# The moments of a residual one slot later, and the row scale behind the first four maxima of the next graph

## The reference

```
q, k, v = x @ Wq.T, x @ Wk.T, x @ Wv.T + bv            # split into 12 heads
scores  = q k^T * 384**-0.5 + (adj + adj)
scores  = where(any(scores != 0, over keys), scores, -inf)
p       = nan_to_num(softmax(scores))
out     = (p @ v) @ Wo.T + bo
result  = layernorm(x + out)                           # no gain, no shift
```

## Time and profile before

| | us |
|---|---|
| median of 3 runs (lowest, highest) | 638.47 (637.63, 639.18) |
| the profiled execution | 637.14 |
| its span, first to last instruction | 635.4 |
| PE, DVE, ACT, POOL busy | 593.0, 482.7, 497.6, 452.6 |
| mean granted TensorE clock | 0.993 |

### The profile page before, as it was taken

How to read it: one execution, slowest core, us unless ns; L and a number is a source line. 1 busy time by engine, 2 the same in 40 slices (tenths; PEclk the granted TensorE clock), 3 DMA queues, 4 the chain that set the end, 5 groups by cost and what they waited for, 6 DMA issues and landing times.

```text
span 635.4 us, 23731 instructions
## 1 busy us (share of the span) xinstructions
PE 593.0 (93%) x8448; PEld 518.5 (82%) x8448; DVE 482.7 (76%) x2380; ACT 497.6 (78%) x1975; POOL 452.6 (71%) x691
## 2 busy tenths in 40 slices
PE   8899999999999999999999999999999999999773
PEld 5788888888888888888888888888878888888663
DVE  4778877877877877877877877777887787787884
ACT  5688778778788778778878877877878878877882
POOL 1577777777687687778768678777768768667773
PEclk9999999999999999999999999999999999999998
DMA  8311324232142422224242132423214222112221
GB/s 305 134 37 46 109 85 137 75 110 84 47 134 87 125 84 64 95 82 135 84 126 81 39 121 86 132 80 91 91 58 135 86 75 86 52 52 86 87 79 50
DMA packets 34749, 59.63 MB, mean 94 GB/s; under 512 B 10568, under 2 KB 24008, under 8 KB 34632
## 3 DMA queue, kind: packets, MB, share of 16 engines
q1 hardware_dynamic: 34200, 57.53, 28.1%
q10 hardware_dynamic: 432, 0.59, 0.3%
HBM read 44.50 MB, written 13.62 MB: 91 GB/s over the span
## 4 chain that ended last, share of the span: by engine, by line
PE 74%; DVE 19%; issue 3%; DMA 3%; ACT 0%; POOLq 0%; POOL 0%; DVEq 0%
PE qk_ps L339 32%; PE scores_ps L430 16%; PE v_ps L373 15%; PE scores_ps L360 9%; DVE y L639 6%; DVE stats L642 5%; DVE att_n L626 5%; DMA scale_t<-scale_mem 2%; PE scores_ps L442 1%; DMA scale_mem<-scale_rows 1%; DMA x_raw<-xt 1%; DVE nscores L558 1%; DVE mean_var L644 0%; PE v_ps L442 0%; PE qk_ps L442 0%
## 5 line engine op out<-in xcount | busy, mean ns | idle before, releaser
L473 ACT ACTIVATE probs<-nscores,neg_max 128x128 f32<-128x128 f32 x768 | 297.5, 389 | 34.7 <-DVE neg_max L558 34.7
L287 POOL TENSOR_TENSOR tree<-nscores 128x512 f32<-128x512 f32 (+1 forms) x128 | 143.1, 1118 | 115.1 <-DVE neg_max L558 115.1
L558 DVE CUSTOM_DVE_ANT_0 nscores<-scores_ps,adj_n 128x128 f32<-128x128 f32 x768 | 171.9, 286 | 4.0 <-PE scores_ps L360 1.7
L473 ACT ACTIVATION_READ_ACCUMULATOR probs<-nscores,neg_max 128x1 f32 x768 | 144.0, 187 | 0.0
L287 POOL TENSOR_TENSOR tree<-tree 128x128 f32<-128x128 f32 (+2 forms) x256 | 127.8, 499 | 20.1
L639 DVE TENSOR_TENSOR y<-scores_ps,x_n 128x384 f32<-128x384 f32 x64 | 35.7, 558 | 110.2 <-PE scores_ps L430 110.2
L430 PE MATMUL scores_ps<-w_o,att_t 128*128 128x384 f32 x576 | 112.8, 341 | 7.1 <-DVE att_t L630 4.6
L373 PE MATMUL v_ps<-w_v,x_t 128*128 128x384 f32 x576 | 111.7, 338 | 1.1 <-ACT probs_t L498 1.1
L339 PE MATMUL qk_ps<-x_t,w_k 128*128 128x512 f32 (+1 forms) x540 | 108.9, 346 | 0.0
L373 PEld LDWEIGHTS v_ps<-w_v,x_t 128*128 128x128 f32 x576 | 102.2, 188 | 7.4 <-ACT probs_t L498 1.9
L339 PE MATMUL qk_ps<-x_t,w_q 128*128 128x512 f32 (+1 forms) x540 | 107.5, 343 | 0.0
(11 more groups left out here) (71 smaller groups left out, 928.0 us busy)
## 6 DMA issues: line engine op xcount, KB each, us to landing
x_n<-xn SPq DMA_DIRECT2D x32, 384.0 KB, 4.8
scale_t<-scale_mem SPq DMA_DIRECT2D x63, 192.0 KB
out<-out_n SPq DMA_DIRECT2D x31, 384.0 KB, 2.6
x_raw<-xt SPq DMA_DIRECT2D x15, 768.0 KB, 5.4
adj_n<-adj SPq DMA_DIRECT2D x32, 128.0 KB, 4.4
scale_mem<-scale_rows SPq DMA_DIRECT2D x63, 16.0 KB
x_raw<-xt SPq DMA_DIRECT2D x3, 256.0 KB, 4.8
nscores<-wq ACTq DMA_DIRECT2D x3, 192.0 KB, 4.2
```

What stands on the lines that cost most here:

```text
L287: nc.gpsimd.tensor_tensor(tree[:, b % 2, low:high, 0:width], src[:, :, 0:width], src[:, :, width:2 * width], ALU.add).then_inc(tree_step, 1)
L473: last = nc.scalar.activation(probs[:, b % 2, h], nscores[:, b % 2, h], ACT.Exp, bias=neg_max[:, b % 2, h:h + 1], scale=-1.0, accum_out=ro ...
L558: last = nc.vector.tensor_tensor_reduce(out=nscores[:, half, h], in0=scores_ps[j][:, m * P:(m + 1) * P], in1=adj_n[:, b // 2 % 2, half], s ...
```

## The change

Three edits, all on VectorE:

- The two instructions that find the moments of y leave `residual(b)` and become `moments(b)`, called one slot later, behind `find_scale`. The last two graphs have theirs right behind their residuals.
- `bias_and_max(b + 1, 0)`, the first four maxima of the next graph, comes ahead of `find_scale(b)`.
- `total` and `nonzero` are views with a stride of two elements of buffers twice as long.

```diff
-        total = sb("total", [P, HEADS])
-        nonzero = sb("nonzero", [P, HEADS])
+        total = sb("total", [P, HEADS, 2])[:, :, 0]
+        nonzero = sb("nonzero", [P, HEADS, 2])[:, :, 0]
...
                 nc.vector.tensor_tensor(y[:, half], out_bank(b)[:, 0:HID], x_n[:, b // 2 % 2, half],
                                         ALU.add).then_inc(y_ready, 1)
+
+            def moments(b):
+                half = b % 2
                 dve.wait_ge(y_ready, b + 1)
                 nc.vector.bn_stats(stats[:], y[:, half]).then_inc(stats_done, 1)
                 dve.wait_ge(stats_done, b + 1)
...
             for b in range(-1, NB + 1):
                 if has(b - 1):
                     normalise(b - 1)
+                if has(b + 1):
+                    bias_and_max(b + 1, 0)
                 if has(b):
                     find_scale(b)
+                if has(b - 2) and has(b):
+                    moments(b - 2)
                 if has(b + 1):
-                    bias_and_max(b + 1, 0)
                     bias_and_max(b + 1, 1)
                 if has(b - 1):
                     attention_low(b - 1)
...
                         residual(b - 1)
                 elif b == NB:
                     residual(b - 2)
+                    moments(b - 2)
                     residual(b - 1)
+                    moments(b - 1)
```

More of the change, by code:

```diff
@@ L588, in find_scale @@
                 dve.wait_ge(tree_step, STEPS * (b + 1))
-                nc.vector.reduce_sum(total[:], tree[:, half, :, 0:REST], axis=mybir.AxisListType.X).then_inc(total_done, 1)
+                nc.vector.reduce_sum(total, tree[:, half, :, 0:REST], axis=mybir.AxisListType.X).then_inc(total_done, 1)
                 dve.wait_ge(total_done, b + 1)
-                nc.vector.scalar_tensor_tensor(out=nonzero[:], in0=neg_max[:, half], scalar=0.0, in1=total[:],
+                nc.vector.scalar_tensor_tensor(out=nonzero, in0=neg_max[:, half], scalar=0.0, in1=total,
                                                op0=ALU.not_equal, op1=ALU.max).then_inc(nonzero_done, 1)
@@ L601, in find_scale @@
                         out=scale_n[:].rearrange("p (h d) -> p h d", h=HEADS),
-                        in0=nonzero[:].unsqueeze(2).to_broadcast([P, HEADS, D]), scalar=0.0,
+                        in0=nonzero.unsqueeze(2).to_broadcast([P, HEADS, D]), scalar=0.0,
                         in1=recip[:].unsqueeze(2).to_broadcast([P, HEADS, D]),
@@ L608, in find_scale @@
                 nc.vector.scalar_tensor_tensor(out=row_scale[:, 0:HEADS].rearrange("p (j m) -> p m j", m=KT),
-                                               in0=nonzero[:].rearrange("p (m j) -> p m j", m=KT), scalar=0.0,
+                                               in0=nonzero.rearrange("p (m j) -> p m j", m=KT), scalar=0.0,
                                                in1=recip[:].rearrange("p (m j) -> p m j", m=KT),
```

## The result

The changed kernel takes 718.85 us (median of 4 runs, 718.26 to 722.14) against 638.05 before: a ratio of 1.128, 95% interval 1.125 to 1.132. Two more comparisons of the same pair gave 716.42 (1.122, interval 1.120 to 1.124) and 716.19 (1.121, 1.115 to 1.127). The forecast was 700 with a range of 688 to 715, so the direction and the cause held and the size did not: 62 us were forecast and 81 (78 and 78 in the repeats) came.

What follows compares the result with a forecast made beforehand. The loop through DRAM was taken as the bound: 3.81 + 6.53 = 10.34 us a slot, +58.8 us over 62 intervals, +2.0 head, +0.7 end, giving a span of 696.9 and a time of 700 us; range 688 to 715.

Steps and rivals of the forecast that it cites:

- TensorE's slot is 9.10 us of its own work: Steady slot before the change: 9.47 us, of which 9.10 is TensorE's work and 0.37 waiting for VectorE.
- The scale behind four maxima closes a loop through DRAM that becomes the bound: att_n, scores, four maxima, scale, write, read, att_n: 10.34 us a slot, above TensorE's 9.10, also in the last slots.
- The terms outside the trip, 3.81 us: From att_n to the write's issue: 1.72 us to the maxima, 0.85 for four maxima, 1.24 for find_scale.
- The round trip, 6.53 us: From the issue of the scale's write to DRAM until att_n: 6.85 us in odd slots, 6.2 in even ones.
- the first rival: Write and read through DRAM take longer in steady slots: slot 10.86 us, 732 us; chance 0.09 together with the strides.
- Head and end: First scale later by 2.0 us at the start; moments of graph 61 uncovered in slot 63, 0.7 us.
- The moments give back at most 0.37 us a slot, seen if the loop is open: Moments leave the stretch between y and att_n: at most 0.37 us a slot, ceiling 22.6 us, not seen here.
- The third rival: Scale lands before it is wanted, TensorE alone bounds: 616 us, if write to att_n takes at most 5.29; chance 0.02.
- Strides cost nothing: Two-element strides of total and nonzero on VectorE: nothing counted, at most 14 us kept for the range.
- Another loop through the third maxima: Output projection waits for third maxima behind scale and moments: 8.83 us, under 9.10; near no change, 638; chance 0.01.
- What the profile would show: VectorE waits for scale_t before nearly all 62 att_n; att_n 10.0 and 10.7 us apart in turn; TensorE some 85% busy.
- signs of being wrong: No steady wait on scale_t, a chain through the third maxima, or a lower granted TensorE clock in the new gaps.

Runs made afterwards that it cites:

- moments-alone family: Kernel before with only the moments moved a slot later, behind the scale, scale still ahead of the first maxima: 647.81 us; variants build on it.
- scale-late kernel: Kernel before with only the scale moved behind the first four maxima, moments left in the residual and buffers dense: 713.77 us, ratio 1.120.
- the kernel that gives the maxima's share back: Changed kernel with the scale ahead of the first maxima again, but waiting for the next graph's scores: 684.61 us, ratio 1.070.
- the kernel with quiet transfers: Changed kernel with steady-slot transfers of adj, x_n, output and x_raw cut to next to nothing: 690.71 us, ratio 1.082.
- GpSimd aside: Kernel before with only the moments moved, plus GpSimd waiting for the next scale before its two long additions: 637.16 us, ratio 0.997.

## Why the prediction was right in kind and wrong in size

- *TensorE's slot is 9.10 us of its own work*: right within 0.1 us. Where nothing else held them, slots of the moments-alone family took 9.00 us.
- *The scale behind four maxima closes a loop through DRAM that becomes the bound*: right for the steady slots, where the transfer came last before 50 of the 62 att_n; shown by the scale-late kernel (714 us without the other parts), by the chain, and by the kernel that gives the maxima's share back (685). That it holds in the last slots too was wrong: see below on the third maxima.
- *The terms outside the trip, 3.81 us*: right where the clock was full (3.80 to 3.82 in most slots). The mean is 3.90. In 8 slots the scores took 1.3 to 1.7 us at a lower granted clock, and the forecast had it full from one stretch of 8 us. Over the 62 slots this is 5.4 us.
- *The round trip, 6.53 us*: this is the step that failed. It measured 6.81 (7.03 in odd slots, forecast 6.85; 6.58 in even ones, forecast 6.2), 17.1 us over the 62 slots; in the two other profiles of the same kernel it was 6.71 and 6.75. I sized it from single slots near the end for the odd ones and from two bounds of single slots for the even ones. The 6.2 us is the trip without traffic (6.27 in the kernel with quiet transfers). Of the 0.28 us, 0.11 is the write, 2.05 us against 1.94, and that much the kernel before did show: its mean over 62 slots is 2.11 us, and several slots behind an issue of x_raw had 2.4 to 3.1, such as this one (SP's queue of the kernel before). There it was hidden, and I looked at one slot only. The rest is the read. That x_raw moves only in steady slots, the reason given with the first rival, is not it: in the changed kernel the even slots behind an issue of x_raw have a trip of 6.53 us and the other even ones 6.62, and slots 49 to 58, without x_raw but with projections, have 7.00 in odd and 6.67 in even slots. Which transfer lengthens the read in even slots stays open; in 9 of these 31 att_n waited for TensorE and not for the transfer, and without those the even trip is 6.48.

```profile
253.61 0.43 SPq L250 DMA_DIRECT2D x_raw<-xt  x1
256.12 0.52 SPq L229 DMA_DIRECT2D scale_mem<-scale_rows  x1
259.12 0.53 SPq L233 DMA_DIRECT2D scale_t<-scale_mem  x1
```

- *Head and end*: the first att_n came 1.7 us later (2.0 forecast); from the last att_n with this scale to the end of the span it is 18.0 us, against 16.2 + 0.7 forecast: 1.1 more, in a stretch in which output projections again took twice their time (3.25 us). With 17.1, 5.4 and -0.3 that is 23.3 of the 23.4 us between the forecast span of 696.9 and the measured 720.3.
- *The moments give back at most 0.37 us a slot, seen if the loop is open*: the ceiling was right and the condition wrong. The third rival had the loop open at a trip of 5.29 us for this change; for the moments alone I then counted on 7.4 us of room, and missed that the shift moves `find_scale` under GpSimd's long additions. The scale then leaves 0.65 us later, and in 25 of 62 slots the loop closes again.
- *Strides cost nothing*: right for the access. *Another loop through the third maxima*: dismissed for the whole run, and it bound the last four slots. Its first part was right, 6.62 us forecast from att_n to the output projection and 674.74 - 668.06 = 6.68 measured. The projection behind it was at the lower clock, 2.83 to 3.22 us for 1.58. These four slots are 3.7 us of the 17.1 and 5.4 above.
- *What the profile would show*: att_n 10.56 and 10.85 us apart in the mean (10.0 and 10.7 forecast), TensorE's share 88% (85). The lower granted clock and the chain through the third maxima, both named as signs of being wrong, did come, beside the cause and not in its place.

## What to carry to other kernels

A transfer that is hidden has slack that belongs to it, and an edit that delays its first byte spends it. Work the round trip out as a loop, from the consumer back to itself, before moving anything ahead of its producer, and size it from many slots with the full traffic, step by step, not from one or two. A rival that was far off by its sum can bind where another term, here the clock, changes. When a step leaves the critical path, look also at what its new time runs beside on the engine that was seen to hold it up.

## What the runs showed of the hardware that was not expected

- A VectorE instruction of 12 elements with two SBUF inputs, started while GpSimd ran a tensor addition, ended 0.02 to 0.04 us after it: up to 1.00 us for `row_scale` and 1.31 for `nonzero` instead of 0.18 and 0.17. Instructions with one SBUF input beside it kept their 0.21 and 0.35 us.
- A write of 16 KB to DRAM, 1.94 us when quiet, took 2.0 to 3.1 us with 768 KB issued 2.5 us before it (kernel before) and 3.2 to 4.9 with it issued 1.0 to 2.2 us before (GpSimd aside). A read of 192 KB back, broadcast over partitions, took 4.3 us in the mean with the other transfers cut to next to nothing, and 5.0 with 512 KB queued behind it: what is issued later on the same queue delayed what was issued first. Holding these 512 KB back took odd trips from 7.03 to 6.46 us.
- The granted clock of TensorE fell to the lower level in 13 of the 58 slots with projections, behind gaps of 1.1 to 2.2 us ahead of the scores, and not in others with gaps of up to 1.6 us. It held 1.00 in a stretch of the kernel before in which TensorE was busy for 73% of the time.
